# A fused conditioned feed-forward kernel: the first x_t load on ScalarE's queue, SyncE's weight loads behind the conditioning data, and both passes over down_w one place earlier

## What is computed

```
def reference(x, cond, norm_w, up_w, down_w):       # x (32,256,256), up_w (2048,256), down_w (256,1024)
    scale = cond @ norm_w.T + 1.0
    ms = mean(x * x, axis=-1, keepdims=True)
    h = x * (scale[:, None, :] * rsqrt(ms + 1e-6))
    val, gate = split(h @ up_w.T, 2, axis=-1)
    h = val * gelu(gate, approximate=False)
    hq = act_quant(h)          # per row: round(h * 127/max|h|) and back
    wq = weight_quant(down_w)  # -1, 0, 1 times mean|down_w|, the mean over the whole matrix
    return hq @ wq.T + x
```

## Time and profile before

| | us |
|---|---|
| median of 3 runs | 426.12 |
| lowest, highest | 425.91, 426.13 |
| the profiled execution | 425.97 |
| its span in the trace | 424.2 |
| PE busy | 420.1 |
| DVE busy | 283.4 |
| ACT busy | 186.7 |
| POOL busy | 169.3 |

### The profile page before, as it was taken

How to read it: one execution, slowest core, us unless ns; L and a number is a source line. 1 busy time by engine, 2 the same in 40 slices (tenths; PEclk the granted TensorE clock), 3 DMA queues, 4 the chain that set the end, 5 groups by cost and what they waited for, 6 DMA issues and landing times.

```text
span 424.2 us, 7696 instructions
## 1 busy us (share of the span) xinstructions
PE 420.1 (99%) x2087; PEld 338.7 (80%) x2087; DVE 283.4 (67%) x540; ACT 186.7 (44%) x335; POOL 169.3 (40%) x323
## 2 busy tenths in 40 slices
PE   9999999999999999999999999999999999999997
PEld 6878878888788888888888887887878888788776
DVE  4887765747756577565766657576574775657676
ACT  6745443534435254353434525344353543525441
POOL 2534542524425344353424525254252442534320
PEclk9999999999999999999999999999999999999999
DMA  8614442542435433353433425333254242543324
GB/s 269 209 32 110 135 99 74 148 99 74 99 74 148 99 88 88 91 148 81 112 86 107 115 74 144 80 97 99 74 148 99 74 99 74 148 99 89 84 51 125
DMA packets 82520, 45.01 MB, mean 106 GB/s; under 512 B 68560, under 2 KB 69328, under 8 KB 82384
## 3 DMA queue, kind: packets, MB, share of 16 engines
q1 hardware_dynamic: 82080, 44.47, 40.5%
q10 hardware_dynamic: 432, 0.46, 0.4%
HBM read 20.00 MB, written 8.39 MB: 67 GB/s over the span
## 4 chain that ended last, share of the span: by engine, by line
PE 96%; DVE 2%; DMA 1%; issue 0%; SPq 0%; ACT 0%; DVEq 0%; ACTq 0%
PE p_val L797 40%; PE p_gate L797 40%; PE p_y L817 13%; DMA xt_in<-x_t 1%; DVE h L650 0%; DVE down_tmp L526 0%; PE p_gate L722 0%; DVE h_max L593 0%; DVE y_sb L546 0%; PE p_gate L734 0%; PE p_gate L728 0%; PE p_val L776 0%; PE p_val L775 0%; PE p_val L734 0%; PE p_val L722 0%
## 5 line engine op out<-in xcount | busy, mean ns | idle before, releaser
L650 DVE SCALAR_TENSOR_TENSOR h<-p_val,rstd,gelu 128x512 f32<-128x512 f32 x124 | 92.5, 746 | 118.4 <-PE p_val L797 116.2
L442 ACT ACTIVATE gelu<-p_gate,rstd 128x512 f32<-128x512 f32 x124 | 85.0, 685 | 138.9 <-PE p_gate L797 131.5
L314 POOL TENSOR_TENSOR mean_sq_eps<-mean_sq,rms_eps 128x1 f32<-128x1 f32 x64 | 12.9, 202 | 228.5 <-ACT squares L376 228.5
L388 ACT ACTIVATE q<-q_rounded 128x1024 bf16<-128x1024 f32 x63 | 66.6, 1058 | 85.1 <-DVE q_rounded L607 85.1
L797 PE MATMUL p_gate<-up_hi,a_lo 128*128 128x512 f32 x248 | 79.2, 400 | 0.0
L797 PE MATMUL p_val<-up_hi,a_lo 128*128 128x512 f32 x248 | 78.0, 395 | 0.3 <-DVE h L650 0.3
L797 PE MATMUL p_val<-up_hi,a_hi 128*128 128x512 f32 x248 | 77.9, 395 | 0.0
L797 PE MATMUL p_gate<-up_lo,a_hi 128*128 128x512 f32 x248 | 77.9, 395 | 0.0
L797 PE MATMUL p_val<-up_lo,a_hi 128*128 128x512 f32 x248 | 77.9, 395 | 0.0
L797 PE MATMUL p_gate<-up_hi,a_hi 128*128 128x512 f32 x248 | 77.9, 395 | 0.0
L593 DVE TENSOR_REDUCE h_max<-h 128x1 f32<-128x1024 f32 x63 | 76.7, 1217 | 1.6
(11 more groups left out here) (87 smaller groups left out, 251.1 us busy)
## 6 DMA issues: line engine op xcount, KB each, us to landing
xt_in<-x_t SPq DMA_DIRECT2D x32, 256.0 KB, 2.8
x_all<-x SPq DMA_DIRECT2D x32, 256.0 KB, 2.8
out<-y_sb SPq DMA_DIRECT2D x30, 256.0 KB, 2.2
up_raw<-up_w_t SPq DMA_DIRECT2D x7, 256.0 KB, 5.4
down_raw<-down_w_t SPq DMA_DIRECT2D x1, 1024.0 KB, 7.9
q_t<-q SPq DMA_TRANSPOSE x63, 3.1
up_raw<-up_w_t ACTq DMA_DIRECT2D x1, 256.0 KB, 2.9
out<-y_sb SPq DMA_DIRECT2D x2, 128.0 KB, 1.8
```

What stands on the lines that cost most here:

```text
L314: pool.tensor_tensor(mean_sq_eps[:, j:j + 1], mean_sq[:, j:j + 1], rms_eps[:, :], ALU.add).then_inc(pool_step, 1)
L388: act.activation(q[j % 2][:, :], q_rounded[j % 2][:, :], ACT.Copy, bias=-ROUND).then_inc(q_ready, 1)
L442: act.activation(gelu[c][:, :], p_gate[c][:, :], ACT.Gelu, scale=rstd[:, j:j + 1]).then_inc(gelu_done, 1)
L650: nc.vector.scalar_tensor_tensor(h[s][:, c * W:(c + 1) * W], p_val[c][:, :], rstd[:, j:j + 1], gelu[c][:, :], op0=ALU.mult, op1=ALU.mult). ...
```

## The change

Three edits. First, the first `x_t` is no longer issued by SP but by ACT, behind weight piece (0,0) and ahead of the load of its function table. Second, SP issues the conditioning data and then waits until it has landed, before it issues weight piece (0,1) and all that follows. Third, on DVE `ternary(0)` moves from behind `h` of tile 2, block 1, to behind `h` of tile 2, block 0; `ternary(1)` stays behind `h` of tile 3, block 0; the rescales of tiles 0, 1 and 2, which stood before that, all come behind `ternary(1)`.

```diff
@@ SP
-            load_xt(0, 0)
+            sp.wait_ge(cond_norm_in, 16)
             load_up(0, 1)
             load_up(1, 0)
             load_up(1, 1)
@@ ACT
             act.dma_start(up_raw[:, 0, 0, :], up_w_t[0, 0, :, 0, :]).then_inc(up_in[0], 16)
+            act.dma_start(xt_in[0][:, :, :, :].rearrange("p k j q -> p (k j q)"),
+                          x_t[0].rearrange("p k j q -> p (k j q)")).then_inc(xt_landed[0], 16)
             act.preload_act_table(ACT.Gelu)
@@ DVE
-                        if first and j == TPB and c == 1:
-                            ternary(0)
-                            for done in range(TPB):
+                        if first and c == 0:
+                            ternary(j - TPB)
+                        if first and j == TPB + 1 and c == 0:
+                            for done in range(TPB + 1):
                                 rescale(0, done)
-                        if first and j == TPB + 1 and c == 0:
-                            ternary(1)
...
-                    if j > 0:
+                    if j > 0 and not (first and j == TPB):
                         rescale(u, j)
```

## The result

The changed kernel takes 427.24 us, the median of nine runs (426.88 to 427.61), and the kernel before, on the same chip, 426.06 (nine runs, 425.78 to 426.24). The ratio is 1.0029, with a 95% interval of 1.0021 to 1.0037: slower by 1.18 us, more than the 0.85 that can be told from no change, and outside the predicted 425.1 to 426.2. The profiled execution took 427.17, with a span of 425.3, against a span of 424.2 before.

What follows compares the result with a forecast made beforehand. PE was taken to bound the kernel (96% of the span). 0.62 for DVE plus 0 for the start, off 425.97, gave 425.35; held to the median, 425.5 us (425.3 to 425.7 at 0.60; full range 425.1 to 426.2).

Steps and rivals of the forecast that it cites:

- DVE's move: DVE, tiles 2 and 3: `h` of tile 3, block 0, comes earlier, ending PE's stall near 29.5; 0.62 us gained.
- The cap on the start: First gate product: earlier x_t moves it from 5.49 to 5.23 at best, where PE's fillers end; at most 0.35 us.
- the gain is lost again at block 1 of tile 0: Tile 0's second block waits on weight landings taken as unchanged, so the gain at the start was set to 0.
- The wait on SP: Opening: SP issues piece (0,1) and all behind it 1.0 us later, but landings were taken as unchanged; cost 0.
- full delay of SP: Other end of the start's estimate: SP's whole delay of 1.0 us reaches the landings of the weights.
- the slow rival: Opening: the wait costs its whole 1.0 us, 0.9 to 1.0 lost, 426.45 in all; 0.15 with everything between.
- ACT's load of x_t covers the hole: Opening: argument that x_t's load on ACT's queue keeps the DMA engines from running dry while SP waits.
- The fast rival: Opening: later weights also land 0.3 earlier and the start keeps its 0.3, giving 425.2; chance 0.17.
- Not what it says: DVE: late `mean_abs` holds back `ternary(0)`, so the 0.62 stall stays or only moves, 426.1; chance 0.08.

Runs made afterwards that it cites:

- kernel 1: The kernel before with only the third edit (ternary(0) earlier, rescales behind ternary(1)), all loads as before; 425.58 us, ratio 0.9984.
- kernel 3: The changed kernel with x_t back on SP's queue, issued ahead of SP's wait; 426.83 us, ratio 1.0015.
- kernel 5: The changed kernel with one more instruction on SP, an increment of a semaphore that nobody reads; 426.8 us, ratio 1.0017.
- kernel 6: kernel 1 with SP's wait on the conditioning data added behind weight piece (0,1), ahead of (1,0); 426.2 us, ratio 1.0001.
- kernel 12: kernel 5 with weight piece (0,1) moved to ACT's queue behind x_t and one more unread increment on SP; 426.13 us, ratio 1.0006.
- kernel 4: The changed kernel without SP's wait on the conditioning data, x_t still on ACT's queue; 428.25 us, ratio 1.005.
- 7: kernel 1 with SP's wait on the conditioning data added behind three weight pieces, ahead of x; 425.6 us, ratio 0.9991.
- 9: kernel 1 with ACT's first gelu moved ahead of its `up_hi` (2,1) step; 425.68 us, ratio 0.9993.
- 10: kernel 1 with one more instruction on SP, an unread semaphore increment behind the conditioning data's load; 425.3 us, ratio 0.9984.

## Why the prediction was wrong

**DVE's move: right.** 0.62 was forecast from the chain and 0.56 measured (kernel 1). The pass starts right behind `h`, `h` of tile 3 ends over 1 us before PE needs it, the hole is gone, and nothing new is late. This held in the changed kernel too, although everything there came 1.1 later.

**The cap on the start: right for x_t, wrong for PE.** `a_hi` was put at 4.65 and stands at 4.77; the first product was put at 5.23 and stands at 5.33. But the 5.23 was the end of the fillers, 4.22 + 1.01, taken from one row; they took 1.46, and the second pair of products began at 6.29, later than before. In the 13 profiled executions with six fillers they took 0.84 to 1.46. That the gain is lost again at block 1 of tile 0 was right as well.

**The wait on SP: the step that failed.** It read: "by 5.7 they must have moved the same four first loads in either order, so what delays the stream is only time in which they run dry. [...] ACT's two loads end near 4.0. So I take landings unchanged". What it put at nothing, the wait, measures 1.25 (kernel 3 against kernel 1). Piece (0,1) was put at 5.7 and landed at 6.3; piece (2,0), put at 9.15 as before, landed near 10.3. It was wrong three times over. First, the conditioning data took 2.4 from issue, not 1.9, and over the kernels anything from 1.8 to 2.8; in every kernel where SP really waits that difference goes straight to SP (the issue at 2.60 in kernel 5, 3.18 in kernel 3 and here). I had one row for that transfer, and took it for a constant. Secondly, the first byte came about 1.0 after SP's issue, so the new stream starts at 4.2, not 3.8, while in 4:5 the engines are down to 0.74 busy and 176 GB/s. Thirdly, even then the rate does not return: 6:7 and 7:8 are low again, 135 thousand bytes between them. The end that I had kept as "full delay of SP", and the slow rival with its third pair at 7.4 and block 1 at 12.1, described what happened (7.04 and 12.26). I gave it 0.15, together with everything between. The argument against it ("ACT's load of x_t covers the hole") compared bytes moved by 5.7 and overlooked that the landing that binds is that of (2,0), at 9 to 10 us. Its issue moved by 1.35 and its landing by 1.2. Whether it is late because fewer bytes were moved or because it was issued later is not shown (experiments 6 and 12).

**The end of the program: not in the sum at all.** Even the slow rival gave 426.45. I costed each moved issue by its time on the queue, and by who stands behind it. That SP's stream of instructions becomes one shorter, and that this shifts a load of code by 0.9 us relative to the last stores, was no term and no rival. It cost some 0.4 (0.44 by medians, kernel 5 against the changed one), and lies 420 us away from the edit.

**The fast rival** (x_t no longer shares, later weights come 0.3 earlier) is ruled out: with the wait, x_t's move brings nothing (kernel 5, at 426.8, equals kernel 3, at 426.83), and without the wait it loses nearly 2 us (kernel 4). The rule of the Trainium skill's page "DMA: Bandwidth & Descriptors", section "Issuing engines are not separate DMA queues", that a second issuing engine saves only issue time, agrees with the first of these. The loss in kernel 4 it does not state. **Not what it says** didn't occur: `mean_abs` was there when DVE asked for it.

Still open: why the DMA engines move little a second time, at 6 to 8 us. By 6.9 SP and ACT had issued some 2640 KB and by 7 only about 1290 thousand bytes were moved, so queued work there was. Of the 359 thousand bytes that the changed kernel lacks by 9 us, 172 are missing in 4:5 and 165 from 6 to 9. The dip shows in kernels 3, 5 and 6 and in both traces of the changed one, and not before or in kernel 1; no run here takes it apart. In 6:7 the engines are busy for 0.97 of the time and move 207, so there they are slow and not idle.

## What to carry to other kernels

Before a queue is held back, find the first landing behind it that has no slack, and take the delay of its issue as what the wait can cost. That other queues cover the hole is not enough: in kernel 6 the DMA engines stayed full in 4:5, and over half of the cost stayed. Price a moved load at the spread of its landing over several executions, not at one row. And where a change of a few tenths is judged, look at the last stores: an instruction more or less on a queue can shift a code load into them, so compare with a variant that has the same number of instructions.

## What was not expected of the hardware

An 80 KB load, the first of the program, landed 1.8 to 2.8 us from its issue in different kernels with the same instructions ahead of it. x_t, 256 KB, on ACT's queue landed after 3.0 to 3.5 us while SP waited, after 4.3 with a second load behind it on ACT's queue (kernel 12), and after 4.1 and 5.3 with SP issuing at the same time; on SP's own queue, ahead of the weights, the same load took 3.3 to 3.8 (kernels 1, 3, 6, 7, 9, 10 and the earlier trace rows). A load of 8 KB of code among the last stores goes with a last store that lands in 2.4 instead of 1.8 us, and with 0.28 us of traffic at a sixteenth of the rate at the end. The same six filler matmuls took 0.84 to 1.46 us, at a granted clock of 1.0. Two executions fell far out, 1079.56 us in kernel 4 and 460.56 in the kernel before, with no cause seen.
